# Local attention units: products with the values in groups of two pairs, and eight buffers of exponentials

## The chip, the cores and the metric

The kernel runs on one core of a Trainium2 chip. The metric is the device time of one execution in microseconds (us); lower is better. The engines are TensorE (PE, with its weight loads shown apart as PEld), VectorE (DVE), ScalarE (ACT), GpSimd (POOL) and SyncE (SP), which here only issues DMAs. Each runs its own instructions in order and waits on semaphores for the others.

## What is computed

One transformer block pair over 8 sequences of 512 tokens with 128 features and 16 heads of width 8. The first layer is **local attention**: a token sees itself and the 128 tokens before it. The second is causal attention followed by a mixture of 8 experts, of which each token takes 2.

```python
# layer 1, "local"
allowed = (j <= i) & (j >= i - WINDOW)            # WINDOW = 128
scores = jnp.where(allowed, q @ k.T * HEAD_DIM**-0.5, -jnp.inf)
x = layernorm(x + softmax(scores) @ v @ w_out.T)
# layer 2, "causal", with the mixture of experts
x = layernorm(x + block(x))    # causal attention, then top-2 of 8 experts
```

## The kernel before, in words

A **unit** is one sequence in one of the two attention layers: units 0 to 7 are the local ones, 8 to 15 the causal ones. After them comes a phase with the experts' blocks and the final normalisation, which has no exponentials.

The scores of a unit are cut into **pairs**: a pair fills one `pair_ps` tile of two PSUM banks (128 x 1024 float32). A local unit has 14 pairs, 7 for each half of the heads; a causal unit has 20, 5 for each of four head groups (`score_pair`, `PAIRS`). Two heads' rows lie in the two halves of the partitions, so that a score matmul uses 50 of 64 rows of the array (line 1425).

A unit is also an **iteration** of 14 (local) or 20 (causal) **steps**. All five engines run the same loop over iterations and steps, each with its own share of the work, and what PE does in step k of unit u is written out in one order:

1. `scores(u, k)`, line 1425: the scores of pair k;
2. `maxima(...)`, lines 1450 and 1459 (local) or 1476 and 1482 (causal): one or two tiles of scores of a later unit, from which DVE takes the row maxima (line 929, 933, or 938 to 943). They belong to unit u+1 in steps 0 to 10 of a local unit and to unit u+2 in steps 11 to 13;
3. `times_v(...)`, line 1502: the **products with the values** of exponentials made some steps before. They are float32, in array tiles of 128 rows by 32 columns, four column tiles side by side, and accumulate in `o_ps`, one bank of `side_ps`. A local pair is 4 matmuls of 256 columns (8 of 128 in the seventh and fourteenth pair); the profile counts each float32 matmul twice, so it shows x8 or x16;
4. jobs at fixed steps of a local unit, each behind the products of its step: in step 0 the projection of unit u+2 (line 1523), in step 1 the values of unit u+1 (line 1531), in step 3 the transposes of the unit before (`turn_o`, line 1549), in step 5 `turn_on` (1556), in step 7 the output projection (1562), in step 11 `turn_shift` for unit u+1 (1569).

All `scores`, `maxima`, projection and `turn_o` tiles share a **ring of three** `pair_ps` tiles (`RING`, `wait_ring`): a new one waits until ACT or DVE has read the one three places before it. ACT reads a score tile with one exponential (line 762) into one of `PROBS` = 4 buffers of `probs`; POOL then zeroes what lies outside the mask, in two instructions or one (lines 647, 649, 652), and increments `masked`. `times_v` waits for `masked` of its last pair and increments `pv_done` once for each group. The exponential of pair n waits for `pv_done` of the group that held pair n - 4. ACT copies the finished `o_ps` of a half of the heads to SBUF (`copy_o`, line 770): the first half in step 9, the second in step 2 of the next unit. The first group of a half waits for the copy before it.

`values_of` says which pairs form a group: in a local unit each pair is its own group, 14 groups; in a causal unit the groups are of 2, 2 and 1 pairs. `value_step` says in which step a group is issued: two steps after its last pair, or three for the first group of a half in a local unit. That puts the local groups at steps 3, 3, 4, 5, 6, 7, 8 and 10, 10, 11, 12, 13, then 0 and 1 of the next unit.

A unit's first scores (step 0) wait for a DMA of `shift_t` into the `arena` stacks (SP, line 510). It ends a chain: last maxima tile (step 10), row maxima on DVE, `split_shift` on DVE (lines 956, 958), `turn_shift` on PE in step 11, `take_shift` on ACT (line 840), the DMA. The maxima of step 11 wait for the stacks of unit u+2, which DMAs bring through DRAM (line 489).

Of the kernel before, what the change touches and what calls it, by code (L numbers as in the profile page):

```python
# [16 lines left out]
B, T, C = 8, 512, 128  # L17
# [61 lines left out]
VROW = VPAD + H * VHEAD  # L79
STACKS = 3  # L80
RING = 3
PROBS = 4

STACK_LOADS = 5 * TILES_R * 16
SHIFT_LOADS = 2 * 16
# [2 lines left out]
def head(gs, r):  # L88

    g, s = gs // 2, gs % 2  # L90
    return 8 * (g // 2) + 2 * (2 * s + r) + g % 2


def layer(u):
    return LOCAL if u < B else CAUSAL
# [35 lines left out]
def score_pair(kind, k):  # L131

    if kind == LOCAL:
        half, j = k // 7, k % 7
        if j < 6:
            g = 2 * half + j // 3
            return [(2 * g + s, j % 3, j % 3 * P, 2 * P, s * 2 * P) for s in range(2)]
        return [(4 * half + n, 3, 3 * P, P, n * P) for n in range(4)]
    g, k = k // 5, k % 5
    if k < 2:  # L140
        return [(2 * g + k, 0, 0, T, 0)]
    if k < 4:
        return [(2 * g + k - 2, 1, P, 3 * P, 0), (2 * g + k - 2, 3, 3 * P, P, 3 * P)]
    return [(2 * g + s, 2, 2 * P, 2 * P, s * 2 * P) for s in range(2)]


def values_of(kind):

    if kind == LOCAL:
        return [(k,) for k in range(14)]  # L150
    return [tuple(5 * g + k for k in ks) for g in range(4) for ks in ((0, 1), (2, 3), (4,))]


VALUES = {kind: values_of(kind) for kind in (LOCAL, CAUSAL)}
VALUES_BEFORE = [sum(len(VALUES[layer(v)]) for v in range(u)) for u in range(UNITS + 1)]
VALUES_ALL = VALUES_BEFORE[UNITS]
# [94 lines left out]
def build(nc, x_t_in, x_in, w_in_all, pack_in, out):  # L251
    ctx = ExitStack()
    with ctx:
        def sb(name, shape, dt=F32):
            return ctx.enter_context(nc.sbuf_tensor(name, shape, dt))
# [33 lines left out]
        shift_t = sb("shift_t", [4 * GS, T], BF16)  # L289
        probs = sb("probs", [P, PROBS, 2 * T])  # L290
        o_t = sb("o_t", [P, 2, T])
# [45 lines left out]
        sizes = (E * SEG_BLOCKS, RUNS * RUNS, BLOCKS, LATE_BLOCKS, LATE_BLOCKS * RUNS, 2 * EARLY_BLOCKS)  # L337
# [90 lines left out]
        def final(n, width):  # L428

            return final_sb[:, n * B * NT:(n + width) * B * NT].rearrange("p (t w) -> p t w", w=width)  # L430

        final_stats, final_mean, final_var, final_rstd, final_negmean = final(0, 6), final(6, 2), final(8, 1), final(9, 1), final(10, 1)
        halves = final(11, 1)
# [141 lines left out]
        def _(pool):  # L575
# [64 lines left out]
            def mask(u, k):  # L640

                n = BEFORE[u] + k
                pool.wait_ge(exp_done, n + 1)
                blocks = probs[:, n % PROBS, :].rearrange("p (n q) -> p n q", q=P)
                if layer(u) == LOCAL:
# [107 lines left out]
        def _(act):  # L753
            def exponent(u, k):

                n = BEFORE[u] + k
                act.wait_ge(score_filled, n + 1)
                old = n - PROBS
                if old >= 0:
                    v = next(v for v in (u, u - 1) if v >= 0 and BEFORE[v] <= old)  # L760
                    act.wait_ge(pv_done, VALUES_BEFORE[v] + VALUE_OF_PAIR[layer(v)][old - BEFORE[v]] + 1)
                nc.scalar.activation(probs[:, n % PROBS, :], pair_ps[RING_AT["score", n][0]][:, :, :].rearrange("p b t -> p (b t)"),  # L762
                                     ACT.Exp, scale=SCALE).then_inc(exp_done, 1)
# [632 lines left out]
        def _(pe):  # L1396
# [89 lines left out]
            def times_v(u, n):  # L1486

                kind = layer(u)
                pairs = VALUES[kind][n]
                pe.wait_ge(masked, BEFORE[u] + pairs[-1] + 1)  # L1490
                if n == 0:
                    pe.wait_ge(misc_taken, JOB["v", u])
                half, within = n // HALF_VALUES[kind], n % HALF_VALUES[kind]
                if within == 0 and 2 * u + half:
                    pe.wait_ge(o_copied, 2 * u + half)
                work = sorted(((gs, j, q0, width, col, r, (BEFORE[u] + k) % PROBS) for k in pairs
                               for gs, j, q0, width, col in score_pair(kind, k) for r in range(TILES_R)),
                              key=lambda piece: (piece[1], piece[0] // 2))
                for gs, j, q0, width, col, r, slot in work:
                    g, c, h = gs // 2, 2 * (gs % 2) + r, head(gs, r)  # L1500
                    first = VHEAD * h + (VPAD if g % 2 == 0 else 0)
                    last = nc.tensor.matmul(o_ps[c * VHEAD:(c + 1) * VHEAD, q0:q0 + width], v_aug[u % 2][:, j, first:first + VHEAD],  # L1502
                                            probs[:, slot, r * T + col:r * T + col + width], start=(within == 0), stop=False,
                                            skip_group_check=True)
                last.then_inc(pv_done, 1)

            def turn_h(u):
# [88 lines left out]
            for it in ITERATIONS:  # L1596
                for k in range(steps(it)):
# [7 lines left out]
                    for u, n in values_at(it, k):  # L1605
                        times_v(u, n)
# [63 lines left out]
            for m in range(BLOCKS + Y_LAG):  # L1670
                if m == CHAIN["turn"]:
                    turn_o(LAST)
                if m == CHAIN["on"]:
                    turn_on(LAST)
                if m == CHAIN["out"]:
                    pe.wait_ge(misc_taken, JOB["out", LAST] - 1)
                    out_project(LAST)
                if m == CHAIN["xf"]:
                    turn_moe(LAST)
                if m == CHAIN["logits"]:  # L1680
                    pe.wait_ge(misc_taken, JOB["logits", LAST] - 1)
                    gate(LAST)
                if m == CHAIN["rank"]:
                    pe.wait_ge(misc_taken, JOB["rank", LAST] - 1)
                    rank(LAST)
                if m == EARLY_BLOCKS + Y_LAG:
                    pe.wait_ge(planned, 2)
                for n in second_at(m):
                    if starts_group(n):
                        expert_of.update(words(block_expert, n, group_end(n), mybir.EngineType.PE, E - 1))  # L1690
                if m < BLOCKS:
                    turn_block(m)
                if H_LAG <= m < BLOCKS + H_LAG:
                    first_layer(m - H_LAG)
                for n in second_at(m):
                    second_layer(n, expert_of[n])
                if m in CHAIN["values"]:
                    times_v(LAST, len(VALUES[CAUSAL]) - 2 + m)
# [29 lines left out]
```

## Time and profile before

| | us |
|---|---|
| median of 3 runs | 763.76 |
| lowest and highest of them | 757.85, 768.12 |
| the profiled execution | 760.87 |
| its span in the trace | 759.1 |
| mean granted TensorE clock in it | 0.939 of full |

| engine | busy us | share of the span |
|---|---|---|
| PE | 627.7 | 83% |
| DVE | 565.8 | 75% |
| ACT | 463.0 | 61% |
| POOL | 420.9 | 55% |

Busy time is time in which the engine worked on an instruction; matmuls overlap each other and the ends of PE's are modelled. The local units fill about the first 278 us of the span, the causal ones end at about 567 us, and the experts' blocks and the final normalisation take the rest. In the trace's timeline the bracket after a row is the idle time of the engine before it and what ended it; "issue" there is a wait for nothing that the profile shows.

### The profile page before, as it was taken

How to read it: one execution, taken by the hardware profiler on the slowest of the kernel's cores; microseconds unless marked ns; L12 is line 12 of the kernel's file. 1: busy time of each engine (PE TensorE's matmuls, PEld its weight loads, DVE VectorE, ACT ScalarE, POOL GpSimd, SP SyncE). 2: the span in 40 equal slices, each digit the busy share in tenths (PEclk: the TensorE clock that was granted, in tenths of full speed). 3: DMA queues.
4: the chain of work that ended last, by engine and by line, in shares of the span. 5: the costliest groups of instructions: out<-in, count | busy, mean ns of one | idle time of the engine just before them, and what ended most of it. 6: DMA issues, size and time to landing. Idle time of an engine off the chain costs nothing.

```text
span 759.1 us, 20439 instructions
## 1 busy us (share of the span) xinstructions
PE 627.7 (83%) x7679; PEld 386.6 (51%) x7679; DVE 565.8 (75%) x1265; ACT 463.0 (61%) x774; POOL 420.9 (55%) x646
## 2 busy tenths in 40 slices
PE   3568998999988788998889888889677996999960
PEld 1333544544544443444444434444226996999950
DVE  2565786888878889898989888988633775566656
ACT  3046775777766476767676767666763573456534
POOL 5026666667765454244647464757755545555753
PEclk9569998999999999999999999999978998899985
DMA  6744843754652627263536363621221223222645
GB/s 199 188 122 98 196 140 60 196 143 105 137 149 53 165 77 149 85 118 106 138 104 140 106 139 89 155 63 26 62 60 43 68 61 88 72 68 75 138 94 166
DMA packets 59004, 84.31 MB, mean 111 GB/s; under 512 B 7848, under 2 KB 48272, under 8 KB 55836
## 3 DMA queue, kind: packets, MB, share of 16 engines
q1 hardware_dynamic: 52284, 68.78, 35.9%
q0 software_dynamic: 6336, 13.71, 7.6%
q8 instruction: 62, 1.02, 0.6%
q10 hardware_dynamic: 288, 0.52, 0.2%
q14 instruction: 34, 0.28, 0.2%
HBM read 43.55 MB, written 37.17 MB: 106 GB/s over the span
## 4 chain that ended last, share of the span: by engine, by line
PE 49%; DVE 16%; issue 9%; DMA 8%; ACT 8%; POOL 4%; SPq 3%; another core or an unknown queue 1%; POOLq 0%; ACTq 0%; DVEq 0%
PE side_ps L1502 10%; PE pair_ps L1651 8%; PE pair_ps L1663 8%; ACT probs L762 5%; PE pair_ps L1425 5%; DMA arena<-parts_dram 5%; DVE row_max L938 4%; PE pair_ps L1523 4%; DVE row_max L940 2%; PE pair_ps L1482 2%; PE side_ps L1562 2%; DMA arena<-shift_t 2%; PE pair_ps L1476 2%; SPq L489 2%; POOL rows_dram L672 2%
## 5 line engine op out<-in xcount | busy, mean ns | idle before, releaser
L762 ACT ACTIVATE probs<-pair_ps 128x1024 f32<-128x1024 f32 x272 | 275.9, 1022 | 125.5 <-PE pair_ps L1425 117.5
L1502 PE MATMUL side_ps<-probs,v_aug 128*32 128x256 f32 (+3 forms) x2048 | 161.0, 410 | 9.1 <-POOL probs L660 4.1
L889 ACT ACTIVATE arena<-pair_ps,arena 128x128 f32<-128x128 f32 x284 | 81.0, 369 | 77.8 <-PE pair_ps L1651 45.8
L647 POOL TENSOR_SCALAR_AFFINE_SELECT probs<-probs 128x512 f32<-128x512 f32 x96 | 61.4, 640 | 112.2 <-ACT probs L762 111.3
L1425 PE MATMUL pair_ps<-arena 50*128 50x256 bf16 (+3 forms) x1024 | 107.2, 285 | 19.5 <-DMA arena<-shift_t 7.1
L929 DVE TENSOR_REDUCE row_max<-pair_ps 128x4 f32<-128x768 f32 x96 | 89.1, 950 | 27.2 <-PE pair_ps L1459 26.7
L713 POOL DMA_INDIRECT outputs_dram<-arena x71 | 70.9, 999 | 66.8 <-DVE arena L1293 35.2
L1651 PE MATMUL pair_ps<-arena 128*128 128x128 f32 x568 | 80.3, 287 | 11.5 <-DVE arena L1282 7.2
L1425 PEld LDWEIGHTS pair_ps<-arena 50*128 50x128 bf16 x1024 | 32.3, 95 | 99.5 <-issue 46.7
L938 DVE TENSOR_REDUCE row_max<-pair_ps 128x2 f32<-128x1024 f32 x64 | 76.7, 1219 | 8.3 <-PE pair_ps L1482 5.9
L1663 PE MATMUL pair_ps<-pack,arena 128*128 x568 | 78.2, 283 | 3.8 <-ACT arena L889 3.2
L1502 PEld LDWEIGHTS side_ps<-probs,v_aug 128*32 128x32 f32 x2048 | 47.9, 109 | 62.9 <-issue 36.7
L1651 PEld LDWEIGHTS pair_ps<-arena 128*128 128x128 f32 x568 | 73.2, 202 | 13.2 <-issue 12.1
L940 DVE TENSOR_REDUCE row_max<-pair_ps 128x8 f32<-128x1024 f32 x64 | 77.6, 1219 | 3.1 <-PE pair_ps L1482 3.1
L1663 PEld LDWEIGHTS pair_ps<-pack,arena 128*128 128x128 f32 x568 | 72.4, 200 | 4.1 <-issue 4.1
L672 POOL DMA_INDIRECT rows_dram<-rows,row_at x64 | 64.2, 1003 | 17.6 <-issue 15.1
L1476 PE MATMUL pair_ps<-first_b,eye_b 64*128 64x128 bf16 (+2 forms) x640 | 48.4, 229 | 22.9 <-ACT probs L762 12.3
L1482 PE MATMUL pair_ps<-arena 48*128 48x128 bf16 (+3 forms) x512 | 61.5, 297 | 0.0
L649 POOL TENSOR_SCALAR_AFFINE_SELECT probs<-probs 128x512 f32<-128x512 f32 x96 | 61.2, 637 | 0.0
L1291 DVE TENSOR_TENSOR arena<-pair_ps,pack 128x128 f32<-128x128 f32 x71 | 20.6, 290 | 52.0 <-PE pair_ps L1663 26.2
L658 POOL TENSOR_SCALAR_AFFINE_SELECT probs<-probs 128x256 f32<-128x256 f32 x64 | 27.0, 422 | 47.4 <-ACT probs L762 46.2
L1450 PE MATMUL pair_ps<-window_b,ident_b 64*64 64x256 bf16 x384 | 30.9, 312 | 26.2 <-DMA arena<-parts_dram 19.2
(178 smaller groups left out, 1007.6 us busy)
## 6 DMA issues: line engine op xcount, KB each, us to landing
arena<-parts_dram SPq DMA_DIRECT2D x96, 192.0 KB
parts_dram<-parts SPq DMA_DIRECT2D x32, 384.0 KB
parts_dram<-parts SPq DMA_DIRECT2D x32, 256.0 KB
pack<-in_pack SPq DMA_DIRECT2D x8, 578.0 KB, 10.0
arena<-rows_dram SPq DMA_DIRECT2D x71, 65.0 KB
parts_dram<-parts SPq DMA_DIRECT2D x32, 128.0 KB
arena<-parts_dram SPq DMA_DIRECT2D x32, 128.0 KB
resid<-outputs_dram POOLq DMA_DIRECT2D x6, 512.0 KB
```

What stands on the lines that cost most here:

```text
L672: nc.gpsimd.indirect_dma_start(out=table[:, :], out_offset=bass.IndirectOffsetOnAxis(ap=row_at[:, j:j + 1], axis=0), in_=rows[:, j // NT, ...
L713: nc.gpsimd.indirect_dma_start(out=outputs[:, :], out_offset=bass.IndirectOffsetOnAxis(ap=place, axis=0), in_=block_y[n % Y_DEPTH], in_off ...
L762: nc.scalar.activation(probs[:, n % PROBS, :], pair_ps[RING_AT["score", n][0]][:, :, :].rearrange("p b t -> p (b t)"), ACT.Exp, scale=SCAL ...
L889: last = nc.scalar.activation(hidden[n % H_DEPTH][:, f * BLK:(f + 1) * BLK], hidden_ps[n % 2][:, f * BLK:(f + 1) * BLK], ACT.Gelu_apprx_ta ...
L929: nc.vector.tensor_reduce(top[:, i, :, 2 * g:2 * g + 2], pair[:, :, 0:2 * WIN].rearrange("p b (s k) -> p b s k", k=WIN), AX_X, ALU.max).th ...
L938: nc.vector.tensor_reduce(top[:, 3, :, 2 * g + m], pair[:, :, :], AX_X, ALU.max).then_inc(max_done, 1)
L940: nc.vector.tensor_reduce(top[:, 0:3 * NT + 1:NT, :, 2 * g + m - 2], pair[:, :, :].rearrange("p b (n k) -> p n b k", k=P), AX_X, ALU.max). ...
L1425: last = nc.tensor.matmul(pair[:, r, col:col + width], k_st[u % STACKS][own, gs, j * P:(j + 1) * P], q_st[u % STACKS][own, gs, q0:q0 + wid ...
L1482: last = nc.tensor.matmul(pair[:, r, col:col + keys], qs[own, gs, i * P:(i + 1) * P], ks[own, gs, 0:keys], start=False, stop=(n == len(wor ...
L1502: last = nc.tensor.matmul(o_ps[c * VHEAD:(c + 1) * VHEAD, q0:q0 + width], v_aug[u % 2][:, j, first:first + VHEAD], probs[:, slot, r * T + ...
L1651: last = nc.tensor.matmul(hidden_ps[n % 2][:, f * BLK:(f + 1) * BLK], block_w[n % W_DEPTH][:, PACK_W1 + f * P:PACK_W1 + (f + 1) * P], bloc ...
L1663: last = nc.tensor.matmul(y_ps[n % 2][:, 0:C], hidden[n % H_DEPTH][:, f * BLK:(f + 1) * BLK], pack[:, bass.ds(expert, 1), PACK_W2 + f * C: ...
```

## The change

`LOCAL_GROUPS` puts the seven pairs of each half of the heads in a local unit into groups of 2, 2, 2 and 1, so that a local unit has 8 groups in place of 14. By the unchanged `value_step` they are issued at steps 4, 5, 7, 8 and 11, 12, then 0 and 1 of the next unit (pairs 0 and 1 at step 4, 2 and 3 at step 5, 4 and 5 at step 7, 6 at step 8, 7 and 8 at step 11, 9 and 10 at step 12, 11 and 12 at step 0, 13 at step 1). `times_v` sets the start flag only on the first matmul that a column tile of `o_ps` gets in a half, since a group can now hold two matmuls for it. `probs` has 8 buffers in place of 4, and the exponential of pair n waits for the group that held pair n - 8. The causal units keep their groups; the final phase uses the first four buffers as before.

```diff
--- before.py
+++ after.py
@@ -79,7 +79,7 @@
 VROW = VPAD + H * VHEAD
 STACKS = 3
 RING = 3
-PROBS = 4
+PROBS = 8
 
 STACK_LOADS = 5 * TILES_R * 16
 SHIFT_LOADS = 2 * 16
@@ -144,10 +144,17 @@
     return [(2 * g + s, 2, 2 * P, 2 * P, s * 2 * P) for s in range(2)]
 
 
+LOCAL_GROUPS = (2, 2, 2, 1)
+
+
+def grouped(halves, pairs, sizes):
+    return [tuple(range(pairs * half + sum(sizes[:i]), pairs * half + sum(sizes[:i + 1]))) for half in range(halves) for i in range(len(sizes))]
+
+
 def values_of(kind):
 
     if kind == LOCAL:
-        return [(k,) for k in range(14)]
+        return grouped(2, 7, LOCAL_GROUPS)
     return [tuple(5 * g + k for k in ks) for g in range(4) for ks in ((0, 1), (2, 3), (4,))]
 
 
@@ -1496,12 +1503,14 @@
                 work = sorted(((gs, j, q0, width, col, r, (BEFORE[u] + k) % PROBS) for k in pairs
                                for gs, j, q0, width, col in score_pair(kind, k) for r in range(TILES_R)),
                               key=lambda piece: (piece[1], piece[0] // 2))
+                begun = set()
                 for gs, j, q0, width, col, r, slot in work:
                     g, c, h = gs // 2, 2 * (gs % 2) + r, head(gs, r)
                     first = VHEAD * h + (VPAD if g % 2 == 0 else 0)
                     last = nc.tensor.matmul(o_ps[c * VHEAD:(c + 1) * VHEAD, q0:q0 + width], v_aug[u % 2][:, j, first:first + VHEAD],
-                                            probs[:, slot, r * T + col:r * T + col + width], start=(within == 0), stop=False,
-                                            skip_group_check=True)
+                                            probs[:, slot, r * T + col:r * T + col + width], start=(within == 0 and c not in begun),
+                                            stop=False, skip_group_check=True)
+                    begun.add(c)
                 last.then_inc(pv_done, 1)
 
             def turn_h(u):
```

## Rows read from the trace of the kernel before

**Rows 1.** The page: the span and, from its fifth part, the products with the values.

```profile
span 759.1 us, 20439 instructions
...
L1502 PE MATMUL side_ps<-probs,v_aug 128*32 128x256 f32 (+3 forms) x2048 | 161.0, 410 | 9.1 <-POOL probs L660 4.1
```

**Rows 2.** Stretch, length, busy (instructions) of PE, PEld, DVE, ACT, POOL; clock, DMA, GB/s.

```profile
54.00:75.00 21.00, 17.26 (x331) 8.23 (x324) 13.25 (x15) 12.74 (x14) 15.10 (x24) 1.00 0.57 129
...
101.66:132.20 30.54, 27.63 (x413) 13.83 (x412) 21.98 (x38) 18.51 (x22) 18.99 (x28) 0.89 0.51 123
...
158.77:185.35 26.58, 24.62 (x413) 12.92 (x412) 22.24 (x38) 18.51 (x22) 18.42 (x28) 1.00 0.57 142
```

**Rows 3.** The exponentials, line 762: what ended ACT's idle time before them (us, times).

```profile
  PE pair_ps L1425: 117.5, 120
...
  PE side_ps L1502: 2.0, 3
```

**Rows 4.** Timeline (start, us, engine, line, tile shape), local unit: two pairs, then one.

```profile
164.08 1.07 PE L1502 MATMUL side_ps<-probs,v_aug 128*32 128x256 f32 x16
...
165.09 1.09 PE L1549 MATMUL pair_ps<-ident,o_t 128*128 128x128 f32 x8
...
171.50 0.64 PE L1502 MATMUL side_ps<-probs,v_aug 128*32 128x256 f32 x8
172.07 0.97 PEld L1562 LDWEIGHTS side_ps<-weights,o_norm_t 128*128 128x128 f32 x8 [0.41 <-issue]
```

**Rows 5.** The same timeline: steps 0 to 5 of that unit.

```profile
156.24 0.39 PE L1425 MATMUL pair_ps<-arena 50*128 50x256 bf16 x4 [0.97 <-DMA arena<-shift_t]
...
156.96 0.64 PE L1502 MATMUL side_ps<-probs,v_aug 128*32 128x256 f32 x8
...
157.53 1.98 PE L1523 MATMUL pair_ps<-x_t,weights 128*128 128x512 f32 x4
...
163.35 1.81 DVE L929 TENSOR_REDUCE row_max<-pair_ps 128x4 f32<-128x768 f32 x2
...
166.81 0.69 DVE L986 TENSOR_TENSOR o_norm<-pair_ps,inv_sum 128x512 f32<-128x512 f32 x1
...
167.56 0.39 PE L1425 MATMUL pair_ps<-arena 50*128 50x256 bf16 x4
```

**Rows 6.** The same timeline: steps 5 to 7.

```profile
169.54 0.60 ACT L817 ACTIVATE o_norm_t<-side_ps 128x512 f32<-128x512 f32 x1 [0.53 <-PE side_ps L1556]
...
170.03 2.16 ACT L762 ACTIVATE probs<-pair_ps 128x1024 f32<-128x1024 f32 x2
...
171.10 0.30 PE L1450 MATMUL pair_ps<-window_b,ident_b 64*64 64x256 bf16 x4
...
172.07 1.16 PE L1562 MATMUL side_ps<-weights,o_norm_t 128*128 128x128 f32 x8
```

**Rows 7.** Timeline of the same unit: step 10 to the next unit's start.

```profile
176.30 1.03 ACT L762 ACTIVATE probs<-pair_ps 128x1024 f32<-128x1024 f32 x1
...
178.15 0.54 DVE L958 SCALAR_TENSOR_TENSOR shift<-row_max,shift 128x64 bf16<-128x64 f32 x1
...
178.84 0.38 PE L1569 MATMUL side_ps<-ident_b,shift 128*32 128x128 bf16 x4
...
182.82 0.39 PE L1425 MATMUL pair_ps<-arena 50*128 50x256 bf16 x4 [0.97 <-DMA arena<-shift_t]
```

**Rows 8.** Timeline of the first local unit and of the last.

```profile
67.67 0.30 PE L1450 MATMUL pair_ps<-window_b,ident_b 64*64 64x256 bf16 x4 [2.53 <-DMA arena<-parts_dram]
...
261.96 0.69 DVE L997 TENSOR_TENSOR y<-side_ps,x_tok 128x512 f32<-128x512 f32 x1 [0.44 <-PE side_ps L1562]
```

**Rows 9.** Busy time and granted clock around two of PE's pauses.

```profile
65.00:67.60 2.60, 0.14 (x4) 0.00 (x0) 0.81 (x3) 1.02 (x1) 2.03 (x4) 1.00 0.69 124
...
121.00:123.10 2.10, 0.23 (x6) 0.00 (x0) 0.55 (x2) 0.90 (x1) 1.64 (x3) 1.00 0.06 15
123.10:132.80 9.70, 9.66 (x98) 3.79 (x97) 5.13 (x14) 4.14 (x5) 5.21 (x7) 0.65 0.02 5
```

## The prediction, made before the result was known

> **What bounds the kernel now.** I began with the page's busy times: PE is busy 627.7 of 759.1 us (the table above), and the products with the values are one of its largest groups, 161.0 us in 2048 instructions [rows 1]. Half of them are local, the only ones whose grouping changes, so I read the table by stretches next: in a steady local unit of 26.58 us PE is busy 24.62, DVE 22.24 and ACT 18.51 [rows 2]. PE bounds the local units, but not alone: three ring tiles tie it closely to ACT and DVE. Then I asked what the exponentials wait for: PE's scores 117.5 us in all, the products with the values 2.0 us in three waits [rows 3]. So four buffers hardly bind, and eight alone are worth 2.0 us at most. Last I followed one unit in the timeline, from its first scores at 156.24 to the next unit's at 182.82 [rows 5, 7], 26.58 us.
>
> **What a group costs.** One pair starts at 171.50, and the next job's weights load at 172.07, when the products are through, after an idle 0.41: 0.57 us. Two pairs in a row take 164.08 to 165.09: 1.01 us. So a pair that follows another costs 0.44, and each join saves 0.13 [rows 4]. Pairs 0, 1 and 7, 8 already stand in one step; the change adds four joins per local unit (2 and 3, 4 and 5, 9 and 10, 11 and 12). 4 x 0.13 x 8 units = 4.2 us of PE time.
> The Trainium skill says the same in kind (TensorEngine Tiling, Key Properties: changing the tiling mode drains the engine), and the trace agrees that the switch costs something, at 0.13 us. By that rule alone the sum would be 4.2 us less.
>
> **Where the groups land.** The saving counts only if PE is what everything waits for. I walk the unit again with the new order; scores and maxima together take 0.72 (156.24 to 156.96 [rows 5]), maxima 0.40 (171.10 [rows 6] to 171.50 [rows 4]), so scores 0.32.
> - Step 0. The projection stands behind pairs 11 and 12 (1.01) instead of pair 12 (156.96 to 157.53, 0.57): +0.44. ACT's reads of it, DVE's rest and the values' job hang on it, so step 3 is 0.44 late too.
> - Step 3. Pairs 0 and 1 (164.08 to 165.09) go to step 4. The transposes now wait for the ring, for the first of two reductions that begin at 163.35 and take 1.81 together, some 0.95 each with their overlap: 164.30 + 0.44 = 164.74, say 164.8. They take 1.02, to 165.8; scores 0.32, maxima 0.40, and the group 1.01 end at 167.55. Before, step 5 began at 167.56, held by DVE's division of 166.81 [rows 5]; that now ends near 167.2 and holds nothing. The debt is paid back.
> - Step 5. 167.55 + 0.72 + 1.01 = 169.28 for `turn_on` instead of 167.56 + 0.72 + 0.57 = 168.85: +0.43. ACT's copy of it (169.54) stands before the exponential of step 6 in ACT's queue (170.03), so that is late by 0.43 [rows 6].
> - Steps 6 and 7. Step 6 has no products now, but it doesn't help: the maxima of step 7 reuse the ring tile of the scores of step 6 and wait for that exponential. Before, 171.10; now 170.46 + 1.03 + 0.04 = 171.53. Then 0.40 and a double group of 1.01 instead of 0.40 and 0.57: the output projection starts at 172.94 instead of 172.07 [rows 6], +0.87.
> - Steps 8 to 10. Same order up to the last maxima, all +0.87. Pairs 7 and 8 leave step 10, but DVE, not PE, is next on the chain: `split_shift` ends at 178.69 + 0.87 = 179.56 [rows 7].
> - Step 11. Ahead of `turn_shift` now stand pairs 7 and 8 (1.01) for pair 9 (0.57), but they start earlier: the maxima wait only for the exponential of step 10 (176.30 + 1.03 = 177.33 before [rows 7], now + 0.87). 178.22 + 0.40 + 1.01 = 179.63 against 178.84 before: +0.79. The DMA and the next unit's first scores follow, 182.82 + 0.79 [rows 7].
> PE has more idle time, and less work, than before: 0.52 us less per unit, 0.79 us longer.
>
> **The sum.** Five units run this way (iterations 1 to 5): 5 x 0.79 = 3.95. In the first local unit PE waits 2.53 us at step 11 for the stacks' DMA, which hides all that came before [rows 8]; behind it the double group delays `turn_shift` by 0.44. In the last two the row maxima are the causal units', on a DVE that is nearly full; there DVE waits for the output projection behind a double group (0.44 idle before 261.96 [rows 8]), so I take 0.44 each, between 0 (DVE hides it) and 0.87 (as in the others). Sum 3.95 + 3 x 0.44 = 5.3 us. More buffers: 0 to -2.0, I take 0, since the three waits lie in the causal units and what comes next there is again PE or DVE. A change in the masks' timing costs nothing: POOL has 8 us free per unit (18.42 of 26.58 busy [rows 2]), and each group follows its last mask by as many steps as before; should POOL be late, the price is one mask in a unit, 18.42 / 14 = 1.3 us. The start flag moves no instruction. 760.87 + 5.3 = 766.2 for the profiled execution, which is 2.9 us under the median; for the median 763.76 + 5.3 = **769.1 us**.
>
> **Rivals.**
> 1. *Joined groups save and nothing waits*, -4.2 us, 759.6. For it: PE is busy 93% of a steady unit, and the saving per join is measured. Against it: the walk meets ACT at step 7 and DVE at step 10, waits which are there already.
> 2. *The delays are absorbed*: 0 to 1 us, 764. For it: PE waits 0.97 us for the DMA of `shift_t` before each unit [rows 7], and a shift of 0.4 us could vanish in such waits. Against it: that DMA hangs on the same chain and moves with it.
> 3. *The change does not do what it says*: the buffers never bound, so the second half of it does nothing. That is nearly certain, and is in my sum; if the first half did nothing too, 763.8.
> 4. *The clock falls, slower by over 2%.* Lumped products leave PE more and longer pauses. After a pause near 121 us, PE busy 0.23 of 2.10 us, the granted clock was 0.65 over the next 9.7 us [rows 9], so that part of it ran at 1.2 instead of 2.4 GHz. The unit around it took 30.54 us, 3.96 more than a steady one, of which 1.9 are the pause, 2.1 the clock [rows 2, 9]. Seven such stretches more, one per unit, are 14.7 us: 763.8 + 5.3 + 14.7 = 783.8. It decides from five stretches on (15.3 - 5.3 = 10.0, over 2.1). Against it: a longer pause, 0.14 us of work in 2.60, left the clock at 1.00 in the whole stretch from 54 to 75 us [rows 2, 9], and the pauses that I add are 0.2 to 0.6 us.
> The Trainium skill describes this danger (TensorE: Matmul & The Clock Gate, "A second HAM failure mode: psum-queue depth-cycling": micro-idles between groups of matmuls can make the clock swing). This trace shows steady units with such pauses at 1.00 throughout [rows 2], so it doesn't bear the rule out so far.
>
> **Chances.** The walk's own case, later by 2 to 9 us, 0.55, its own range 764 to 776; rival 1 0.18; rivals 2 and 3 together 0.20; rival 4 0.05; anything that I don't see, half of it on the slow side, 0.02. A measurement of this kernel can tell some 2%, 15.3 us, from no change, and all but rival 4 lie inside that. The runs shown spread by 10 us, which can carry the slowest of the walk's outcomes past the bound. Faster 0.02, within 2% 0.91, slower 0.07. For the range: below, rival 1 with the spread of the runs under it, 757; above, 769.1 with 0.87 in all eight units (+1.7) and three more low stretches of 2.1 us, 777, rounded to 778.
>
> **What would show it.** Timeline of a steady unit after: first scores to first scores 27.2 to 27.5 us in place of 26.58; projection 0.4 later behind step 0; step 5 unchanged; the maxima of step 7 waiting for the exponential; the output projection 0.9 later. Rows of line 1502 the same in number, with joined groups of 1.01 us. ACT's idle time put down to products with the values: none. DVE's and ACT's busy times unchanged. The prediction is wrong if a steady unit takes 26.1 us or less (rival 1), or if the granted clock of the local stretch falls under 0.95.

## The result, and the profile after

The changed kernel took 765.1 us, median of 20 runs (761.42 to 769.27); the kernel before, run beside it, 760.02 us (20 runs, 755.35 to 768.12). The ratio is 1.0069 (95% interval 1.0044 to 1.0093): 5.1 us slower, inside the 2% that counts as no change, and clear of zero. The forecast was 5.3 us more. Its level of 769.1 us stands on the 763.76 of the first three runs of the kernel before; that kernel's 20 runs have a median 3.7 us lower. In a few executions the chip is in a slower state; medians are of all executions, ratios leave the slow ones out (one of six with the groups on four buffers, one of ten with the new steps without groups, one of the kernel before in the second group). The profiled execution has a span of 763.5 us against 759.1.

The page of the changed kernel, its span and its products with the values (line 1510 now), which answer to [rows 1]:

```profile
span 763.5 us, 20435 instructions
...
L1510 PE MATMUL side_ps<-probs,v_aug 128*32 128x256 f32 (+3 forms) x2048 | 156.8, 411 | 9.6 <-POOL probs L667 4.0
```

PE's time in the products fell by 4.2 us (161.0 to 156.8), the four joins of 0.13 us in eight units. The span rose by 4.4 us all the same. What ended ACT's idle time before the exponentials, line 769, as [rows 3]:

```profile
  PE pair_ps L1432: 115.3, 115
...
  PE side_ps L1510: 2.7, 4
```

So the added buffers took no wait away. These waits lie in the causal units, three before and four after, and each lasts 0.68 us with four buffers as with eight. The stretches of [rows 2], the third replaced by a steady unit of the changed kernel (its first scores to the next unit's; columns as there):

```profile
54.00:75.00 21.00, 17.99 (x314) 8.54 (x312) 11.99 (x14) 11.86 (x13) 13.17 (x21) 0.84 0.54 113
101.66:132.20 30.54, 25.78 (x437) 13.96 (x430) 23.00 (x39) 19.05 (x23) 19.64 (x30) 1.00 0.51 123
...
185.32:212.80 27.48, 24.07 (x414) 13.22 (x414) 22.31 (x39) 18.76 (x24) 18.27 (x28) 1.00 0.51 128
```

The steady unit lasts 27.48 us instead of 26.58, with PE busy 24.07 instead of 24.62: less work in more time. The granted clock is 1.00 in it. Low clock lies in the first unit here (0.84) and lay in the third before (0.89); the changed kernel has a further short stretch of it, in the seventh unit.

The same unit in PE's timeline (start, duration, line; first scores at 185.32):

```profile
185.32 0.39 PE L1432 MATMUL pair_ps<-arena 50*128 50x256 bf16 x4 [1.12 <-DMA arena<-shift_t]
...
186.04 1.07 PE L1510 MATMUL side_ps<-probs,v_aug 128*32 128x256 f32 x16
187.04 1.98 PE L1532 MATMUL pair_ps<-x_t,weights 128*128 128x512 f32 x4
...
193.01 0.30 PE L1457 MATMUL pair_ps<-window_b,ident_b 64*64 64x256 bf16 x4 [0.55 <-ACT probs L769]
...
193.95 1.07 PE L1558 MATMUL pair_ps<-ident,o_t 128*128 128x128 f32 x8 [0.47 <-DVE row_max L936]
...
196.67 0.39 PE L1432 MATMUL pair_ps<-arena 50*128 50x256 bf16 x4
...
197.40 1.07 PE L1510 MATMUL side_ps<-probs,v_aug 128*32 128x256 f32 x16
198.40 0.66 PE L1565 MATMUL side_ps<-ident,o_norm 128*128 128x128 f32 x4
...
200.66 0.30 PE L1457 MATMUL pair_ps<-window_b,ident_b 64*64 64x256 bf16 x4 [0.55 <-ACT probs L769]
...
201.06 1.07 PE L1510 MATMUL side_ps<-probs,v_aug 128*32 128x256 f32 x16
202.06 1.16 PE L1571 MATMUL side_ps<-weights,o_norm_t 128*128 128x128 f32 x8
...
207.46 0.30 PE L1457 MATMUL pair_ps<-window_b,ident_b 64*64 64x256 bf16 x4 [0.32 <-ACT probs L769]
...
207.85 1.07 PE L1510 MATMUL side_ps<-probs,v_aug 128*32 128x256 f32 x16
208.82 0.38 PE L1578 MATMUL side_ps<-ident_b,shift 128*32 128x128 bf16 x4
```

In ACT's queue, steps 5 to 7, as in [rows 6]:

```profile
199.09 0.60 ACT L824 ACTIVATE o_norm_t<-side_ps 128x512 f32<-128x512 f32 x1 [0.96 <-PE side_ps L1565]
199.59 1.94 ACT L769 ACTIVATE probs<-pair_ps 128x1024 f32<-128x1024 f32 x2
```

And all engines at the unit's end, as in [rows 7]:

```profile
206.28 1.95 ACT L769 ACTIVATE probs<-pair_ps 128x1024 f32<-128x1024 f32 x2
...
208.13 0.54 DVE L965 SCALAR_TENSOR_TENSOR shift<-row_max,shift 128x64 bf16<-128x64 f32 x1
...
212.80 0.39 PE L1432 MATMUL pair_ps<-arena 50*128 50x256 bf16 x4 [1.13 <-DMA arena<-shift_t]
```

Counted from the unit's first scores, in us, with the walk of the prediction between the two traces:

| | before | forecast | after |
|---|---|---|---|
| projection (step 0) | 1.29 | 1.73 | 1.72 |
| maxima of step 3 | 7.26 | 7.70 | 7.69 |
| `turn_o` | 8.85 | 8.56 | 8.63 |
| scores of step 5 | 11.32 | 11.31 | 11.35 |
| `turn_on` (step 5) | 12.61 | 13.04 | 13.08 |
| exponential of step 6 | 13.79 | 14.22 | 14.27 |
| maxima of step 7 | 14.86 | 15.29 | 15.34 |
| output projection (step 7) | 15.83 | 16.70 | 16.74 |
| end of `split_shift` | 22.45 | 23.32 | 23.35 |
| `turn_shift` (step 11) | 22.60 | 23.39 | 23.50 |
| next unit's first scores | 26.58 | 27.37 | 27.48 |

The reader is to see three things in these rows. The projection starts behind a double group (186.04 to 187.04), 0.43 late; by step 5 that is gone. The maxima of step 7 wait 0.55 us for the exponential, although PE has no products in step 6 now: the idle PE waits for ACT. And the first scores of the next unit still wait for the DMA of `shift_t`, 1.13 us, more than the 0.97 us of [rows 5]: the DMA moved with the chain and hid nothing.

### The profile page after: what moved, and what is told of

It reads as the page before. It is cut to its first block, busy times and chain, and to the rows that moved or that the text cites. A ratio compares the mean times of both kernels' runs of the same rounds, so it can differ in the third digit from the quotient of the medians.

```text
span 763.5 us, 20435 instructions
## 1 busy us (share of the span) xinstructions
PE 621.8 (81%) x7679; PEld 387.4 (51%) x7679; DVE 564.6 (74%) x1265; ACT 461.1 (60%) x774; POOL 419.1 (55%) x646
## 3 DMA queue, kind: packets, MB, share of 16 engines
q8 instruction: 62, 1.02, 0.6%
## 4 chain that ended last, share of the span: by engine, by line
PE 47%; DVE 15%; issue 10%; DMA 10%; ACT 8%; POOL 5%; SPq 3%; another core or an unknown queue 1%; POOLq 0%; DVEq 0%; ACTq 0%
PE side_ps L1510 10%; PE pair_ps L1660 9%; PE pair_ps L1672 8%; DMA arena<-parts_dram 5%; ACT probs L769 5%; PE pair_ps L1432 4%; PE pair_ps L1532 3%; DVE row_max L945 3%; POOL rows_dram L679 2%; DVE row_max L947 2%; DMA rows_dram<-rows,row_at 2%; DMA arena<-shift_t 2%; PE side_ps L1571 2%; PE pair_ps L1489 2%; ACT parts L808 2%
## 5 line engine op out<-in xcount | busy, mean ns | idle before, releaser
L1510 PE MATMUL side_ps<-probs,v_aug 128*32 128x256 f32 (+3 forms) x2048 | 156.8, 411 | 9.6 <-POOL probs L667 4.0
L1510 PEld LDWEIGHTS side_ps<-probs,v_aug 128*32 128x32 f32 x2048 | 50.8, 110 | 66.2 <-issue 38.0
```

## The experiments

Ten kernels, in three groups, each group on one chip together with the kernel before. The chip of the first group ran the kernel before in 760.49 us, those of the others in 737.25 and 738.12, so only ratios are compared across groups. Beside the times I read the steady unit from the trace, which tells 0.4 us apart where the time can't. Units without a further pause of PE repeat to a few hundredths (27.50 and 27.48 us in the changed kernel, 26.58 twice in the one before). Some have such a pause around their steps 9 to 11 and take up to 0.7 us longer (one of 27.70 in the changed kernel); I give them where they matter.

### Eight buffers alone

```diff
 # kernel before
-PROBS = 4
+PROBS = 8
```

> The kernel before with PROBS = 8 in place of 4 and nothing else. My theory (buffers did not bind; only 2.0 us of waits on the products, in causal units): steady local unit 26.6 us, time within 0 to -2 us of the kernel before. Rival (the larger probs tile or its place in SBUF makes something slower): 2 to 5 us more.

Measured: 763.29 us against 760.49, ratio 1.0023 (0.9999 to 1.0048). First scores of two units in a row (bracket: idle before, and what ended it):

```profile
182.43 0.39 PE L1425 MATMUL pair_ps<-arena 50*128 50x256 bf16 x4 [0.97 <-DMA arena<-shift_t]
...
209.01 0.39 PE L1425 MATMUL pair_ps<-arena 50*128 50x256 bf16 x4 [0.97 <-DMA arena<-shift_t]
```

26.58 us, to the hundredth the unit of before. The time is 1.7 us up where I had 0 to -2, and its interval just reaches zero; a cost of 2 to 3 us, the rival's, is not excluded by it. The steady units show no reason for one. The question comes back below.

### The groups with four buffers

```diff
 # changed kernel
-PROBS = 8
+PROBS = 4
```

> The changed kernel with PROBS = 4 in place of 8. My theory: here the buffers do bind: the exponentials of pairs 4, 6, 8 and of 11, 13 must wait for a group that is issued only in the same step or the one before, behind that step's maxima. Carrying the order through gives a steady unit of about 28.7 us against 27.5 with eight, so 7 to 9 us more than the changed kernel, 12 to 14 more than before, and ACT's idle time put down to line 1510 rises from 2.7 us to over 8. Rival (buffers never bind, in either order): as the changed kernel, 5 us over the kernel before.

Measured: 780.67 us, ratio 1.0240 (1.0211 to 1.0269), some 18 us over the kernel before and 13 over the changed one. What ended ACT's idle time before the exponentials, and two of them, for pairs 4 and 11 of one unit:

```profile
  PE pair_ps L1432: 97.0, 100
  PE side_ps L1510: 45.5, 18
```

```profile
207.34 1.94 ACT L769 ACTIVATE probs<-pair_ps 128x1024 f32<-128x1024 f32 x2 [2.50 <-PE side_ps L1510]
...
220.47 1.02 ACT L769 ACTIVATE probs<-pair_ps 128x1024 f32<-128x1024 f32 x1 [1.74 <-PE side_ps L1510]
```

The exponential of pair 4 waited 2.50 us for the group of pairs 0 and 1, that of pair 11 1.74 us for pairs 7 and 8. So in the new order the buffers bind, and eight of them are what keeps the groups from costing 18 us. The direction was mine, the size was larger than my 12 to 14: the undisturbed unit is 29.14 us where I had 28.7.

### The new steps without groups

```diff
 # kernel before, PROBS = 8
+LOCAL_STEPS = (4, 4, 5, 5, 7, 7, 8, 11, 11, 12, 12, 14, 14, 15)
 def value_step(kind, n):
+    if kind == LOCAL:
+        return LOCAL_STEPS[n]
```

Steps 14 and 15 are steps 0 and 1 of the next unit.

> The kernel before with eight buffers and every pair its own group, but issued at the steps of the changed kernel: 4, 4, 5, 5, 7, 7, 8, 11, 11, 12, 12, 0, 0, 1. Two groups of one step stand back to back on PE. My theory (only the steps matter, not the grouping): steady unit 27.5 us, 5 us over the kernel before. Rival (fewer waits and semaphore increments or the order of the matmuls in a group matter): more than 1 us away from the changed kernel, either way.

Measured: 768.66 us, ratio 1.0096 (1.0062 to 1.0130).

```profile
187.04 0.39 PE L1430 MATMUL pair_ps<-arena 50*128 50x256 bf16 x4 [1.13 <-DMA arena<-shift_t]
...
214.52 0.39 PE L1430 MATMUL pair_ps<-arena 50*128 50x256 bf16 x4 [1.14 <-DMA arena<-shift_t]
```

27.48 us, the unit of the changed kernel. Grouping as such (fewer waits and increments, the start flag) does nothing there; what counts is the step in which each pair's products stand. The time came out at 7.3 us over the kernel before, where the changed kernel has 5.1; the two intervals overlap, and I draw nothing from the difference.

### Two of the joins undone

```diff
 # the kernel above
-LOCAL_STEPS = (4, 4, 5, 5, 7, 7, 8, 11, 11, 12, 12, 14, 14, 15)
+LOCAL_STEPS = (4, 4, 5, 5, 6, 7, 8, 11, 11, 12, 12, 13, 14, 15)
```

> As e3_same_steps_single, but pair 4 goes back to step 6 and pair 11 back to step 13, so that steps 0 and 7 hold one pair each; steps 4, 5, 11, 12 still hold two. My theory (the double groups at steps 0 and 7 carry all of the loss, 0.44 us each per unit): steady unit 26.6 us, within 1 us of the kernel before. Rival (every double group costs, since it holds up the scores behind it): a steady unit of 27.0 or more, 2 to 4 us over the kernel before.

Measured: 764.83 us, ratio 1.0058 (1.0028 to 1.0088).

```profile
184.19 0.39 PE L1430 MATMUL pair_ps<-arena 50*128 50x256 bf16 x4 [0.56 <-DMA arena<-shift_t]
...
210.80 0.39 PE L1430 MATMUL pair_ps<-arena 50*128 50x256 bf16 x4 [0.56 <-DMA arena<-shift_t]
```

The steady unit is 26.61 us (the one before it, from 156.93, took 27.26, with a pause of 0.73 us at step 9): with the joins of steps 0 and 7 gone the loss is gone, although steps 4, 5, 11 and 12 still hold two pairs each. The time did not follow: 4.4 us over the kernel before, where I had said 1 at most. That miss is not explained by the steady units. In the one trace that I have, PE waited 3.65 us at step 11 of the first unit for the stacks (2.53 in [rows 8]), and the granted clock between 215 and 283 us was 0.90 where before had 0.97. The lower clock is not of this trace alone: it was 0.936 on average over the twelve runs and 0.942 over the 27 of the kernel before. Among those 27 a run with 0.01 less clock took some 3 us more (a line through their times and clocks), so by this estimate about 2 of the 4.4 us go with the clock. Why it was lower, and what the rest is, stays open.

### Each of the two alone

First pair 11 back at step 13 (step 0 undone), one execution:

```diff
 # the kernel without groups
-LOCAL_STEPS = (4, 4, 5, 5, 7, 7, 8, 11, 11, 12, 12, 14, 14, 15)
+LOCAL_STEPS = (4, 4, 5, 5, 7, 7, 8, 11, 11, 12, 12, 13, 14, 15)
```

> Eight buffers, single groups, at the steps of the changed kernel except that pair 11 is back at step 13, so that step 0 has pair 12 alone (steps 4, 4, 5, 5, 7, 7, 8, 11, 11, 12, 12, 13, 0, 1). One look at the steady unit. My theory (steps 0 and 7 add 0.44 us each, one after the other): 27.0 us, between 26.6 and 27.5. Rivals: only step 0 costs: 26.6; only step 7 costs: 27.5.

```profile
183.40 0.39 PE L1430 MATMUL pair_ps<-arena 50*128 50x256 bf16 x4 [0.56 <-DMA arena<-shift_t]
...
199.71 1.16 PE L1567 MATMUL side_ps<-weights,o_norm_t 128*128 128x128 f32 x8
...
210.44 0.39 PE L1430 MATMUL pair_ps<-arena 50*128 50x256 bf16 x4 [0.57 <-DMA arena<-shift_t]
```

27.04 us (27.03 and 27.04 in the two units before), and the output projection at 16.31 us from the first scores, 0.48 later than the 15.83 of before. So step 7 alone costs 0.43 over the 26.61 of the last kernel, and step 0 on top of it the other 0.44 of the 27.48. Both rivals (only one of them costs) fall by this run.

Then pair 4 back at step 6 (step 7 undone), one execution:

```diff
 # the kernel without groups
-LOCAL_STEPS = (4, 4, 5, 5, 7, 7, 8, 11, 11, 12, 12, 14, 14, 15)
+LOCAL_STEPS = (4, 4, 5, 5, 6, 7, 8, 11, 11, 12, 12, 14, 14, 15)
```

> The counterpart: pair 4 is back at step 6, so that step 7 has pair 5 alone, and step 0 keeps pairs 11 and 12 (steps 4, 4, 5, 5, 6, 7, 8, 11, 11, 12, 12, 0, 0, 1). One look. My theory: steady unit 27.0 us, with the output projection 0.4 to 0.5 us late counted from the unit's first scores, and the exponential of step 6 late by nothing more. Rivals: only step 0 costs: 27.5; only step 7 costs: 26.6.

```profile
129.01 0.39 PE L1430 MATMUL pair_ps<-arena 50*128 50x256 bf16 x4 [1.22 <-DMA arena<-shift_t]
...
130.73 1.98 PE L1528 MATMUL pair_ps<-x_t,weights 128*128 128x512 f32 x4
```

Its projection stands 1.72 us behind the first scores, as in the changed kernel; the output projection, at 145.32, 16.31 behind them. The unit that begins here ended at 156.05, after 27.04 us, with a wait of 0.38 us for the stacks' DMA in it; the next took 27.42 with a pause of 0.46, and the one after that 27.36 with a wait of 0.71 for the stacks. This run agrees with 0.4 to 0.5 us for step 0, but its later units alone would not exclude 27.5; the split rests on the run above.

### Pair 12 where PE waits

```diff
 # kernel before, four buffers
+LOCAL_STEPS = (3, 3, 4, 5, 6, 7, 8, 10, 10, 11, 12, 13, 13, 15)
```

> The kernel before, four buffers, single groups, with pair 12 in step 13 behind pair 11 in place of step 0 of the next unit. PE waits about 1 us there for the DMA of shift_t, so the pair should cost nothing, and step 0 loses its 0.57 us. My theory (what costs is products in the steps where PE sets the pace): steady unit 26.0 us in place of 26.58, 3 to 4 us less than the kernel before. Rival (any double group delays the chain through shift_t or the next scores): 26.6 or more, and no gain.

Measured: 734.91 us against 737.25, ratio 0.9968 (0.9938 to 0.9997), so 2.4 us less (0.2 to 4.6).

```profile
156.15 0.64 PE L1507 MATMUL side_ps<-probs,v_aug 128*32 128x256 f32 x8 [0.25 <-POOL probs L654]
156.88 0.11 PEld L1430 LDWEIGHTS pair_ps<-arena 50*128 50x128 bf16 x4 [0.58 <-DMA arena<-shift_t]
156.89 0.39 PE L1430 MATMUL pair_ps<-arena 50*128 50x256 bf16 x4
...
157.61 1.98 PE L1528 MATMUL pair_ps<-x_t,weights 128*128 128x512 f32 x4
...
182.17 0.64 PE L1507 MATMUL side_ps<-probs,v_aug 128*32 128x256 f32 x8 [0.25 <-POOL probs L654]
182.89 0.39 PE L1430 MATMUL pair_ps<-arena 50*128 50x256 bf16 x4
```

The unit is 26.00 us, 0.58 less than before: the 0.57 us of pair 12 now lie where PE waited for `shift_t`. The first scores (156.89) still come when that DMA lands, as their weight load shows (156.88), but of the former idle 0.97 us most is taken up: 0.25 waiting for pair 12's mask and 0.57 for its products. The projection follows them at 0.72 us. This is the other side of the same finding: products ahead of the projection cost their full length, products in the wait cost nothing that the unit shows.

### Four joins in other steps

```diff
 # kernel before, four buffers
+LOCAL_STEPS = (3, 3, 4, 6, 6, 8, 8, 10, 10, 12, 12, 13, 13, 15)
```

> Four buffers, single groups, the same four joins in number as in the changed kernel at other steps: pairs 3 and 4 in step 6, 5 and 6 in step 8, 9 and 10 in step 12, 11 and 12 in step 13 (all steps: 3, 3, 4, 6, 6, 8, 8, 10, 10, 12, 12, 13, 13, 1). Joins save 0.13 us each and stand behind, not ahead of, the jobs of steps 5, 7 and 11. My theory: steady unit 25.5 us, 5 to 8 us less than the kernel before. Rival (lumps of products cost wherever they stand): steady unit over 26.6.

Measured: 734.29 us against 737.25, ratio 0.9960 (0.9933 to 0.9987). All engines, from one unit's first scores to the next:

```profile
156.85 0.39 PE L1430 MATMUL pair_ps<-arena 50*128 50x256 bf16 x4
...
169.70 2.32 DVE L1037 TENSOR_SCALAR resid<-y,mean_var,rstd 128x128 f32<-128x128 f32 x4
169.71 0.64 POOL L654 TENSOR_SCALAR_AFFINE_SELECT probs<-probs 128x512 f32<-128x512 f32 x1
...
170.59 1.09 POOL L657 TENSOR_SCALAR_AFFINE_SELECT probs<-probs 128x1024 f32<-128x1024 f32 x1 [0.25 <-ACT probs L767]
...
173.01 0.39 PE L1430 MATMUL pair_ps<-arena 50*128 50x256 bf16 x4 [0.49 <-DVE row_max L934]
...
183.09 0.39 PE L1430 MATMUL pair_ps<-arena 50*128 50x256 bf16 x4
```

The steady unit is 26.24 us, not 25.5, and no better than with pair 12 alone; the time is 3.0 us less (1.0 to 4.9) where I had 5 to 8. DVE's scaled copies took 2.32 us for four, and the scores of step 8 waited for the row maxima behind them: the time won on PE turned into a wait for DVE. Of the four copies two are long: the first, begun 0.01 us ahead of a mask on POOL, took 0.73 us beside its 0.64, and the third, begun 0.01 behind the mask of 170.59, took 1.17 beside its 1.09; the other two took 0.33 each. In the kernel before, with pair 12 early and in the last kernel below, the long mask begins when the copies are done, and the four take 1.50. Lumped products do not cost wherever they stand, so the rival falls, but my 25.5 left out DVE.

### Eight buffers again, and pair 5 behind the output projection

```diff
 # kernel with pair 12 early
-PROBS = 4
+PROBS = 8
```

> The kernel of e7_pair12_early with eight buffers in place of four; nothing else. It asks again what eight buffers alone do, since e1 came out at 1.0023 (0.9999 to 1.0048), neither clearly zero nor clearly a cost, with a trace whose steady units were those of the kernel before. If the buffers do nothing: ratio to the kernel before as e7's, 0.9968, within 0.002, and steady units of 26.0 us. If eight buffers cost some 1.8 us outside the steady units (e1's point estimate): ratio 0.999 or more.

Measured: 733.55 us against 738.12, ratio 0.9968 (0.9936 to 1.0000), the ratio of its twin with four buffers (the two against different runs of the kernel before). Two steady units of its one trace took 26.03 and 26.23 us, those of the twin 26.03 and 26.00. I conclude that eight buffers alone neither help nor cost what this measurement can see; by the two intervals, that is to within some 3 us (an estimate).

```diff
 # kernel with pair 12 early, four buffers
-LOCAL_STEPS = (3, 3, 4, 5, 6, 7, 8, 10, 10, 11, 12, 13, 13, 15)
+LOCAL_STEPS = (3, 3, 4, 5, 6, 8, 8, 10, 10, 11, 12, 13, 13, 15)
```

> The kernel of e7_pair12_early (four buffers), with pair 5 moved from step 7 to step 8, where it joins pair 6 (steps 3, 3, 4, 5, 6, 8, 8, 10, 10, 11, 12, 13, 13, 1). The output projection of step 7 then has no products ahead of it, and PE saves one join. My theory: the output projection comes 0.57 us earlier, but the scores behind it meet the row maxima of DVE, as in e8, so that only the join's 0.13 is gained: steady unit 25.9 us, ratio 0.996. Rival (all double groups cost 0.44 ahead of the next scores): 26.4 us.

Measured: 734.74 us against 738.12, ratio 0.9951 (0.9925 to 0.9977). All engines, from one unit's first scores to the next:

```profile
153.87 0.39 PE L1430 MATMUL pair_ps<-arena 50*128 50x256 bf16 x4
...
166.71 1.50 DVE L1037 TENSOR_SCALAR resid<-y,mean_var,rstd 128x128 f32<-128x128 f32 x4
...
168.56 1.16 PE L1567 MATMUL side_ps<-weights,o_norm_t 128*128 128x128 f32 x8
...
179.74 0.39 PE L1430 MATMUL pair_ps<-arena 50*128 50x256 bf16 x4
```

The steady unit is 25.87 us, as expected, and the output projection starts 14.69 us behind the first scores instead of 15.26 in the twin with pair 12 early (172.15 behind 156.89). The wait for DVE's row maxima that I expected behind it did not come: the next scores started at 169.66, as soon as PE was through with the projection. Pair 5 just stands behind the projection instead of ahead of it, and the join's 0.13 is what is left. This kernel is half a per cent under the kernel before, while the changed one is 0.7% over it. That pair 5 adds anything to pair 12 is in the unit (25.87 for 26.00), not in the time: the two intervals overlap almost wholly.

## Why the prediction was right

**What a group costs.** Confirmed: 1.00 us for each double group (186.04 to 187.04), and PE's time in products down by the 4.2 us of the sum.

**Step 0, +0.44.** Measured 0.43, and with pair 11 taken back the unit gets shorter by 0.44 of its 27.48. **Step 3, paid back**: scores of step 5 at 11.35 for 11.31. **Step 5, +0.43**: 0.47. **Steps 6 and 7, +0.87**: 0.91. The exponential of step 6 is late behind ACT's copy, and the maxima of step 7 wait for it, as said.

**Step 11, +0.79.** Mis-sized by 0.11. I let the maxima of step 11 start 0.02 behind the exponential of step 10; they started 0.16 behind its end (207.46, with the exponential at 206.28 and 1.02 long). Unit 27.48 for 27.37.

**The sum.** Five units at 0.90 are 4.5, where I had 3.95. From the second unit's first scores to the seventh's the changed kernel took 139.81 us (72.99 to 212.80) and the one before 136.90 (72.50 to 209.40), 2.9 more, and 5.0 with the 2.1 us added that the prediction puts down to the low clock in the kernel before. The last two local units took 65.58 us against 64.48 (to 278.38 and 273.88, the first scores of the first causal unit), 1.10 more where I had 0.88; each trace has one stretch of 3.4 us at the lower clock in them. At that point the changed kernel is 4.5 us behind, and the spans differ by 4.4: the whole loss lies in the local units. The first unit can't be read cleanly, since the clock of the changed kernel was low in it. These rows are PE around it:

```profile
70.53 1.77 PE L1510 MATMUL side_ps<-probs,v_aug 128*32 128x256 f32 x16
...
74.16 1.07 PE L1510 MATMUL side_ps<-probs,v_aug 128*32 128x256 f32 x16
```

The double group at 70.53 took 1.77 us there, and one at 74.16, at full clock, 1.07. The sum of 5.3 agrees with the measured 5.1, but with an interval of about 3.3 to 7.1 us (0.44% to 0.93%), so the time alone bears out the sign and the order of size; the steady unit bears out its term. That the two totals lie 0.2 us apart is in part luck: the five units cost 0.55 more than forecast, the last two 0.2 more, and the first is not known.

**More buffers, 0.** Borne out in the units (26.58 us alone; 26.03 in both twins), and in the time only to within some 3 us. The bound of -2.0 was misread: the 0.68 us waits that it counted are there with eight buffers too, and "none", the sign that the prediction gave for them, did not come true (2.7 us in four). And the prediction calls the second half of the change idle, as if it could be left out, and that was wrong by 13 us: with the groups and four buffers the kernel is 2.4% slower than before. I had read that four buffers don't bind in the old order, and not asked whether they would in the new one.

**Rival 1** (joins save, nothing waits) fell: PE did save the 4.2 us, and the span rose. **Rival 2** (absorbed by the wait for `shift_t`) fell: that wait grew to 1.13 us. **Rival 3** (the change does nothing) fell: the new order lengthens the unit by 0.90 us, and in that order the buffers are worth 13 us. **Rival 4** (the clock) did not happen: 1.00 in steady units, with PE busy 88% of them instead of 93%; from 54 to 278 us it was 0.98 in both traces. Eleven of the twelve traces show one to three low stretches each between 54 and 234 us, at changing places, so a single one says little on an edit. The saving per join of 0.13 us, beside which the prediction names the drain rule of the Trainium skill (TensorEngine Tiling (Array Packing), Key Properties), came out at its measured size on PE and did not reach the time; whether it is a drain that the join saves, no run here shows.

## What to carry to other kernels

Work that is only gathered must be looked at where it lands: ahead of what in its engine's queue, and whether the engine was waiting there. A double group ahead of a projection costs its length, and in a wait it is free; moving one pair into a wait gained 0.58 us per unit where two badly placed joins lost 0.90. And a buffer count that is idle in one order can be what carries the next, so both halves of a change are to be priced together and apart.

## What the runs showed of the hardware that was not expected

- The kernel before ran in 760.49 us on one chip and in 737.25 and 738.12 us on others. The attention units took the same: ACT's last copy of `o_ps` began at 571.82 us in the trace of before and at 569.72 in that of the kernel with pair 12 early, on the faster chip. What came after it took 187 us of the span there and 164 here. Of this stretch PE was busy 147.7 us at a granted clock of 0.89 in the first trace and 138.4 us at 0.94 in the second. The six traces of the slower runs (before, after and the first group) each show ACT idle there 4 to 7 times, 13 to 23 us in all, until something that the profile does not show; the six others show no such wait. What it is stays open.
- A scaled copy of 128x128 on DVE took 0.33 us by itself, 0.73 when it began together with a mask of 0.64 us on POOL, and 1.17 beside one of 1.09, so it ended within 0.1 us of the mask both times. DVE's row maxima, which read `pair_ps`, took their usual 0.94 us beside the same mask of 1.09. So the order of products on PE moved a mask on POOL onto a copy on DVE: 2.32 us for the four copies instead of 1.50.
